# Two short stretches of weighted values moved beside the stretch behind them, in causal attention with a mixture feed-forward

## What is computed

```python
scores = jnp.einsum('bhqd,bhkd->bhqk', q, k) / jnp.sqrt(jnp.asarray(hd, x.dtype))
causal = jnp.tril(jnp.ones((T, T), bool))
scores = jnp.where(causal, scores, jnp.asarray(-jnp.inf, x.dtype))
attn = jax.nn.softmax(scores, axis=-1)
y = jnp.einsum('bhqk,bhkd->bhqd', attn, v)
```

## Time and profile before

| | us |
|---|---|
| median of 3 runs | 813.16 (812.86 to 813.42) |
| the profiled execution's own time | 813.01 |
| its span (first to last instruction) | 811.2 |
| PE busy | 793.2 (98%) |
| PE weight loads (PEld) | 533.1 (66%) |
| DVE busy | 689.6 (85%) |
| ACT busy | 439.2 (54%) |
| POOL busy | 303.8 (37%) |

### The profile page before, as it was taken

How to read it: one execution, slowest core, us unless ns; L and a number is a source line. 1 busy time by engine, 2 the same in 40 slices (tenths; PEclk the granted TensorE clock), 3 DMA queues, 4 the chain that set the end, 5 groups by cost and what they waited for, 6 DMA issues and landing times.

```text
span 811.2 us, 15794 instructions
## 1 busy us (share of the span) xinstructions
PE 793.2 (98%) x5262; PEld 533.1 (66%) x5262; DVE 689.6 (85%) x2100; ACT 439.2 (54%) x843; POOL 303.8 (37%) x387
## 2 busy tenths in 40 slices
PE   9999999999999999999999999999999999999996
PEld 6788876876545555454555555555458888888885
DVE  4874767678899999999999999999688888888877
ACT  5333322323479988888998888998851111111110
POOL 0213121222223452535436454555442734435321
PEclk9999999999999999999999999999999999999999
DMA  8316183364613444343354445351421101011111
GB/s 292 113 42 200 38 238 100 98 189 107 158 44 68 106 99 93 79 103 89 81 122 107 85 101 114 79 122 43 125 77 47 53 26 52 26 52 42 37 40 39
DMA packets 44097, 75.51 MB, mean 93 GB/s; under 512 B 13372, under 2 KB 14844, under 8 KB 44028
## 3 DMA queue, kind: packets, MB, share of 16 engines
q1 hardware_dynamic: 44028, 74.64, 35.4%
HBM read 48.30 MB, written 21.23 MB: 86 GB/s over the span
## 4 chain that ended last, share of the span: by engine, by line
PE 80%; DVE 8%; ACT 5%; issue 2%; DMA 1%; SPq 1%; POOL 0%; DVEq 0%
PE bank L1854 16%; PE bank L1738 11%; PE bank L1723 11%; PE bank L550 11%; PE bank L552 10%; PE bank L551 10%; ACT pt L1109 4%; PE bank L1667 2%; PE bank L2001 2%; PE bank L1733 1%; PE bank L1683 1%; PE bank L1749 1%; DVE b_low L1369 1%; PE bank L1734 1%; DMA ks<-k_parts 1%
## 5 line engine op out<-in xcount | busy, mean ns | idle before, releaser
L1109 ACT ACTIVATE pt<-bank 128x512 f32<-128x512 f32 x576 | 305.1, 621 | 52.8 <-PE bank L1723 49.9
L1249 DVE CUSTOM_DVE_ANT_0 bank<-bank,cmask 128x256 f32<-128x256 f32 (+3 forms) x456 | 202.8, 491 | 22.0 <-PE bank L1738 20.5
L1723 PE MATMUL bank<-qs,ks 50*128 50x512 f32 (+3 forms) x768 | 206.2, 377 | 1.1
L1738 PE MATMUL bank<-ks,qs 48*128 48x512 f32 (+3 forms) x712 | 190.0, 391 | 2.2 <-DMA ks<-k_parts 1.2
L1738 PEld LDWEIGHTS bank<-ks,qs 48*128 48x128 f32 x712 | 101.0, 185 | 90.7 <-DVE mx L1252 28.1
L1854 PE MATMUL bank<-pt,vb 128*32 128x512 f32 (+3 forms) x1536 | 157.0, 496 | 0.2 <-ACT pt L1109 0.2
L876 POOL TENSOR_SCALAR_AFFINE_SELECT pt<-pt 128x512 f32<-128x512 f32 (+1 forms) x160 | 85.3, 553 | 157.8 <-ACT pt L1109 157.8
L1723 PEld LDWEIGHTS bank<-qs,ks 50*128 50x128 f32 x768 | 114.9, 185 | 36.4 <-ACT pt L1109 25.0
L1252 DVE TENSOR_REDUCE mx<-bank 128x1 f32<-128x512 f32 x200 | 130.6, 679 | 1.4 <-PE bank L1738 1.1
L795 POOL TENSOR_TENSOR part<-rope,part 128x1024 fp32r<-128x1024 f32 x16 | 38.2, 2389 | 164.1 <-ACT part L967 164.1
L921 POOL TENSOR_TENSOR g<-comb,hr 128x1024 f32<-128x1024 f32 x16 | 30.5, 1906 | 110.5 <-DVE comb L1490 105.0
(11 more groups left out here) (194 smaller groups left out, 1535.2 us busy)
## 6 DMA issues: line engine op xcount, KB each, us to landing
qs<-q_parts SPq DMA_DIRECT2D x34, 256.0 KB, 3.9
ks<-k_parts SPq DMA_DIRECT2D x34, 256.0 KB, 4.4
q_parts<-part SPq DMA_DIRECT2D x32, 256.0 KB, 3.5
k_parts<-part SPq DMA_DIRECT2D x32, 256.0 KB, 3.5
qs<-q_parts SPq DMA_DIRECT2D x34, 128.0 KB, 5.0
ks<-k_parts SPq DMA_DIRECT2D x34, 128.0 KB, 3.3
yv<-yts SPq DMA_DIRECT2D x128, 32.0 KB, 2.3
rspread<-dens SPq DMA_DIRECT2D x64, 64.0 KB, 2.3
```

What stands on the lines that cost most here:

```text
L1109: act.activation(pt[k % PT_BUFS][:, h], score_out(g, c), ACT.Exp, scale=float(HD) ** -0.5).then_inc(S("exp_done"), 1)
L1249: last = ve.tensor_tensor_reduce(blk, blk, cmask[:, BANK - nk * P:], 1.0, NEG, ALU.add, ALU.max, mx[m][:, 0, h, qt:qt + 1])
L1723: last = pe.matmul(score_out(g, c)[:, col:col + n_], ks[slot_of(g)][r0:r0 + KX, h // 2, kb * P:(kb + 1) * P], qs[slot_of(g)][r0:r0 + KX, h ...
L1738: last = pe.matmul(out[:, col:col + nk * P], qs[slot][r0:r0 + KR, pr, qt * P:(qt + 1) * P], ks[slot][r0:r0 + KR, pr, k0 * P:(k0 + nk) * P] ...
```

## The change

The change lets two steps have one place and moves step 1 from chunk 12 to chunk 17, where step 2 stands, and step 4 from chunk 25 to chunk 27, where step 5 stands. A group then has eight stretches. The loop in `pe_group` issues all the steps of a place, lowest first.

```diff
-VALUES_AT = [8, 12, 17, 22, 25, 27, 32, 35, 38, 41]
+VALUES_AT = [8, 17, 17, 22, 27, 27, 32, 35, 38, 41]
...
-assert all(a < b for a, b in zip(VALUES_AT, VALUES_AT[1:])) and VALUES_AT[-1] - SCORE_BANKS < VALUES_AT[0]
+assert all(a <= b for a, b in zip(VALUES_AT, VALUES_AT[1:])) and VALUES_AT[-1] - SCORE_BANKS < VALUES_AT[0]
...
                     score(g, c)
-                    if g > 0 and c + SCORE_BANKS in values_at(g - 1):
-                        weighted(g - 1, values_at(g - 1).index(c + SCORE_BANKS))
-                    if c in values_at(g):
-                        weighted(g, values_at(g).index(c))
+                    for i in range(NPV):
+                        if g > 0 and c + SCORE_BANKS == values_at(g - 1)[i]:
+                            weighted(g - 1, i)
+                    for i in range(NPV):
+                        if c == values_at(g)[i]:
+                            weighted(g, i)
```

## The result

The changed kernel takes 833.2 us (median of 4 runs, 831.36 to 834.23) against 813.0 before: a ratio of 1.0248, with a 95% interval of 1.0236 to 1.0260. It is slower, as forecast, by 20.2 us where 10.1 were forecast, and outside the range of 819 to 826. The profiled execution took 831.36, with a span of 829.6.

A forecast was written before the change was run, and what follows sets the result against it. PE, ACT and DVE wait for each other in a ring, so PE time counts only where others wait for it. 0.43 + 0.29 = 0.72 us a group, over 14 groups 10.1 us, gave 823.2 us, range 819 to 826.

The forecast's parts named there:

- ring: Whole group: scores wait for exponentials three chunks back, maxima banks for reads four banks back, tying PE, ACT and DVE together.
- Removing step 1 from chunk 12 gives nothing: Chunk 12: step 1 is off the chain, scores 13 to 17 wait for exponentials 10 to 14; gain zero.
- Place 1: Step 1 from chunk 12 to 17, joined with step 2: PE reaches score 18 0.43 us later per group.
- Place 2: Step 4 from chunk 25 to 27: 0.14 gained, stretch grows by 0.43, net 0.29 us later at score 28.
- The first group: First group: gain of 0.1 to 0.3 at chunk 12's step against 0.29 at the other move, taken as zero.
- The clock: TensorE clock stays at 2.4 GHz; added PE waits, below 1 us, come between matmuls and are priced at nothing.
- PE as the bound: Rival: each of 30 removed stretches saves run-out and entry, 7.8 us in all, giving 805.4 us; chance 0.05.
- only place 1 costs: Rival: earlier exponentials and maxima offset the 0.29 at chunk 28; 14 x 0.43 = 6.0 us, 819.2 us; chance 0.10.
- both places cost more: Rival: 0.43 + 0.43 a group gives 825.2 us, 0.57 + 0.57 gives 829.2; chance 0.12.
- What was to show it: Four profile signs: ACT chain and PE load waits, first joined stretch 1.43, second 1.43, group of 24.66 us.
- My first sign: Exponential 9 to score 16: chain over ACT with the same 3.10 us, PE's weight loads waiting some 0.5 us more.

The follow-up runs named there:

- place 1 alone: Only step 1 moved from chunk 12 to 17, step 4 left at 25, against the kernel before: 827.7 us, ratio 1.0199.
- place 2 alone: Only step 4 moved from chunk 25 to 27, step 1 left at 12, against the kernel before: 818.5 us, ratio 1.0073.
- The doubled scores: Changed kernel with scores 13, 14 and 15 computed twice into the same bank in groups 2 to 15: 824.9 us, ratio 1.0148 to the kernel before.
- all four joins: Kernel before with one pair of steps joined: 1 and 2 (827.7 us), 4 and 5 (818.5), 8 and 9 (826.5), 6 and 7 (822.65).

## Why the prediction was right in its ring and wrong on the clock

- **Removing step 1 from chunk 12 gives nothing: right for the ring.** Score 17 comes as late as before in every group at full clock, and the kernel without step 1 keeps its 23.94 us.
- **Place 1, 0.43 us later: right.** The changed kernel with place 1 alone has groups 0.43 longer. The joined stretch takes 1.43 in the chain.
- **Place 2, 0.29 later: 0.37 measured.** Score 27 came 0.14 to 0.16 earlier as forecast. The missing term is the entry of the stretch: I kept that of before, and it is about 0.09 longer behind a score that starts on an idle PE. It is read from the timeline of several kernels, and was not tested by an experiment of its own.
- **The first group, taken as zero: 0.68 measured.** I had credited it with a gain of 0.1 to 0.3 at place 1 since step 1 was on its chain. Place 1 alone costs 0.26 there and place 2 alone 0.43. DVE has hardly a wait in this group. With place 1 alone its wait behind step 2 is 0.43 longer, and it stands 0.25 later from score 0 on, so the time that PE gained at chunk 12 let DVE run 0.18 ahead and no more. That is read from the two timelines; no experiment tested it.
- **The clock, "I price it at nothing": this is the step that failed.** The prediction said that the added waits of PE stay below 1 us and come between matmuls. They do, and still the clock fell for 3.41 us in 5 groups of the profiled execution. 6.8 us of the missing 8.3 in that execution (18.4 of span against 10.1) are these falls, 1.1 are 14 x 0.08 at place 2, and 0.7 the first group; the attention also begins 0.3 us earlier in this execution. The doubled scores bring 8.4 us back in the median, to 824.9, which lies inside the range of 819 to 826: what took the measured time out of it was the clock. What the runs show in place of the step is this. In the 3.40 us up to the joined stretch no wait of the weight loads is longer than 0.31 us, while the kernel before has one of 0.41 there, behind step 1, and keeps its clock. What changed is the number of matmuls, 16 records for 24. The Trainium skill, TensorE: Matmul & The Clock Gate, Part 1, says that the granted rate follows how busy PE has been recently. The trace agrees: at place 1 the rate falls where PE's work was taken away (16 records) and mostly stays up where it is put back (20). At place 2, where 21 records are left, it stays up too. Short waits between single matmuls were enough, and why some groups fall and others with the same work do not was not tested.
- **The rivals.** PE as the bound is refuted in all four joins, and "only place 1 costs" by the kernel with place 2 alone (818.5). The 824.9 of the doubled scores is near the 825.2 of "both places cost more", but not for its reasons: place 2 did gain its 0.14, and what came on top was the entry and the first group. The rule of the Trainium skill, TensorEngine Tiling (Array Packing), Key Properties, that a change of tiling mode drains the engine, fits the 0.14 that a joined stretch saves (1.43 for 0.57 + 1.00). No run here tells such a drain from the plain run-out of a stretch's last matmuls. Either way it is worth less than what the order costs around it.
- **What was to show it.** The waits of ACT at 0.58 and 1.03 (0.9 forecast) and the two stretches of 1.43 came as said. So did ACT's busy time (21.21); DVE's is 23.19 for 22.8, and place 2 brings the rise (23.14 in the group 410.26 to 434.61 with place 2 alone, 22.85 with place 1 alone), which I can't explain. The weight loads did not wait 0.5 us more from exponential 9 to score 16. They are busy 1.65 us of 3.10 there before and 1.84 after, so they stand still for less time though those of step 1 are gone. I had said of the weight loads that they show PE's waits better than its busy time does; they show single waits, and their sum does not tell how much work PE lost. The chain did not run over ACT from exponential 9 but over PE's scores 13 to 16, each of which waits for an exponential: both ways are equally late there, 3.10 us from 449.11 to 452.21. My first sign was badly chosen, the time between the two ends being the sign that counts.

## What to carry to other kernels

When three engines wait for each other in a ring, ask of each piece of work not what it costs but which wait it fills and which it stands ahead of: moved out of a wait, it gains nothing at its old place and, moved behind another, costs its length there. Work that fills a wait of TensorE can also keep its clock up, so look at the granted clock by window before such a place is emptied and after. Where it falls, a few repeated matmuls inside the wait can bring most of it back at no cost to the path. Count the matmuls there, since PE's busy time and that of its weight loads can both hide that there are fewer.

## What was not expected of the hardware

- The clock falls without any long gap of PE: the waits of its loads were up to 0.31 us behind chunk 12, and 3.41 us at 1.2 GHz followed in 5 of 14 groups. Groups with the same work differ, one falls and the next does not, and a kernel's runs spread with it: by 3 us here (831.4 to 834.2) and by 7 with place 1 alone (824.7 at a mean clock of 0.991 to 831.4 at 0.980), where those of the kernel before spread by 1.
- A fall of 3.41 us costs 1.2 to 1.5 us of a group here, less than half of its length. In the kernel without step 1 both falls lasted 6.83 us and cost 2.5.
- A kernel that leaves out matmuls (819.3) is 6.7 us slower than the same kernel with three of its scores in each group issued twice (812.55).
